# An edge-by-edge graph convolution: the loop's instruction lists are written anew, with the block's sums in two PSUM banks and a stop of the gathers for a convolution five blocks back

## The reference

```
h   = gelu(gelu(edge8 @ W_mlp1 / sqrt(8)) @ W_mlp2 / sqrt(64))     # 8 -> 64 -> 64
w00, w01, w10, w11 = h @ Wp_00, h @ Wp_01, h @ Wp_10, h @ Wp_11     # 4 x 32 radial weights
mid = products of the w's, the source node's 128 features (x[src] @ W1) and 4 edge attributes
n   = segment_sum(mid, edge_dst)                                    # per destination node
y   = c * self(x) + s * (n @ W2)
out = layernorm(x + y)
```

## Time and profile before

| | |
|---|---|
| median of 3 runs | 5393.78 us (5361.47 to 5398.54) |
| the profiled execution's own time | 5384.89 us |
| its span, first to last instruction | 5383.0 us |
| mean granted TensorE clock | 0.767 |
| PE busy | 3296.7 us (61%) |
| PE weight loads busy | 1820.5 us (34%) |
| POOL busy | 3103.5 us (58%) |
| DVE busy | 1881.7 us (35%) |
| ACT busy | 1178.5 us (22%) |

### The profile page before, as it was taken

How to read it: one execution, slowest core, us unless ns; L and a number is a source line. 1 busy time by engine, 2 the same in 40 slices (tenths; PEclk the granted TensorE clock), 3 DMA queues, 4 the chain that set the end, 5 groups by cost and what they waited for, 6 DMA issues and landing times.

```text
span 5383.0 us, 53986 instructions
## 1 busy us (share of the span) xinstructions
PE 3296.7 (61%) x15272; PEld 1820.5 (34%) x15272; DVE 1881.7 (35%) x6401; ACT 1178.5 (22%) x2646; POOL 3103.5 (58%) x3281
## 2 busy tenths in 40 slices
PE   6566655666665665666566555666666665666666
PEld 5333333333333333333333333333333333333334
DVE  2333333333333333333333333333333333333335
ACT  3222122222222221222222222222222222222224
POOL 5466555566655565556655665556565566555651
PEclk8777777777777777777777777777777787778777
DMA  6122112212212122222221221212222122122211
GB/s 152 34 47 46 44 42 44 44 44 47 46 43 46 42 46 44 44 45 45 46 45 43 47 46 42 45 44 46 43 46 45 43 46 46 43 46 45 46 45 60
DMA packets 586055, 256.02 MB, mean 48 GB/s; under 512 B 528383, under 2 KB 531867, under 8 KB 584347
## 3 DMA queue, kind: packets, MB, share of 16 engines
q0 software_dynamic: 103616, 211.52, 15.1%
q1 hardware_dynamic: 480572, 42.82, 6.7%
q10 hardware_dynamic: 1696, 0.18, 0.0%
HBM read 241.45 MB, written 12.81 MB: 47 GB/s over the span
## 4 chain that ended last, share of the span: by engine, by line
another core or an unknown queue 51%; PE 27%; issue 13%; ACT 8%; DVE 0%; ACTq 0%; DMA 0%; DVEq 0%; POOL 0%; POOLq 0%
PE bank L735 6%; PE bank L778 5%; PE bank L730 5%; PE bank L745 5%; PE bank L759 3%; PE bank L770 2%; ACT h L517 2%; ACT big L522 1%; ACT ztsb L543 1%; ACT ztsb L544 1%; PE bank L677 1%; ACT bank L532 1%; ACT idx L501 1%; ACT big L635 1%
## 5 line engine op out<-in xcount | busy, mean ns | idle before, releaser
L436 POOL DMA_INDIRECT gath<-feature_table,idx x3224 | 3077.2, 954 | 2149.6 <-issue 1711.0
L745 PE MATMUL bank<-wpbd,big 128*128 128x256 f32 x3232 | 982.4, 433 | 27.1 <-issue 25.5
L994 DVE TENSOR_TENSOR big<-bank,gath 128x256 f32<-128x256 f32 x808 | 342.2, 424 | 1737.2 <-remote 1481.8
L778 PE MATMUL bank<-ztsb,conv 128*128 128x128 f32 x1616 | 360.4, 392 | 865.4 <-ACT ztsb L544 574.8
L745 PEld LDWEIGHTS bank<-wpbd,big 128*128 128x128 f32 x3232 | 707.5, 225 | 472.5 <-issue 404.1
L997 DVE TENSOR_TENSOR big<-bank,gath 128x384 f32<-128x384 f32 x1616 | 817.9, 548 | 0.0
L770 PE MATMUL bank<-ident,zsb 128*128 128x128 f32 x1616 | 342.8, 351 | 700.3 <-issue 505.4
L735 PE MATMUL bank<-h,w2bd 128*128 128x512 f32 x804 | 571.8, 801 | 232.2 <-ACT h L517 128.0
L1022 DVE TENSOR_TENSOR acc<-acc,bank 128x8 f32 x3232 | 528.7, 164 | 509.4 <-PE bank L778 93.3
L730 PE MATMUL bank<-e8T,w1bd 128*128 128x512 f32 x804 | 571.0, 799 | 156.2 <-ACT big L522 77.6
L778 PEld LDWEIGHTS bank<-ztsb,conv 128*128 128x128 f32 x1616 | 308.1, 285 | 982.5 <-issue 492.6
(11 more groups left out here) (83 smaller groups left out, 799.0 us busy)
## 6 DMA issues: line engine op xcount, KB each, us to landing
gath<-feature_table,idx POOLq DMA_INDIRECT x3224
e<-in_edge_attr SPq DMA_DIRECT2D x416, 32.0 KB
ea_t<-in_edge_attr SPq DMA_DIRECT2D x100, 64.0 KB
feature_table<-gath SPq DMA_DIRECT2D x4, 1280.0 KB, 5.6
out<-big SPq DMA_DIRECT2D x4, 1280.0 KB
big<-in_x SPq DMA_DIRECT2D x3, 1280.0 KB, 8.4
dst_rows<-in_dst SPq DMA_DIRECT2D x1, 1536.0 KB
big<-in_src SPq DMA_DIRECT2D x1, 1408.0 KB
```

The lines of the kernel that those rows point to most:

```text
L436: pool.indirect_dma_start(out=gath[:, s % SLOTS, t, :], out_offset=None, in_=table[:, :], in_offset=bass.IndirectOffsetOnAxis(ap=idx[:, s, ...
L745: last = pe.matmul(wgt_ps[c][:, 256 * r:256 * (r + 1)], h2[:, s // SUPER % 2, s % SUPER, 16 * g:16 * (g + 1), :].rearrange("q p a -> q (p ...
L778: last = pe.matmul(y_ps, conv[:, k, :], ztsb[:, k, :], start=(k == 0), stop=(k == 3))
L994: dve.tensor_tensor(o[:, :, :, 0, :], w[:, :, :, 0, :], f[:, :, 0, :].unsqueeze(2).to_broadcast([128, n, 2, MUL]), ALU.mult)
```

## The change

- **PE** gets a list `cycle` in place of `step`. One cycle b holds, in this order: layer2 (h=1) of the block five ahead, radial chunk 2 of block b+1, layer1 (h=0) of the block six ahead, radial chunk 3 of b+1, all eight transposes of block b-1, layer2 (h=0), radial chunks 0 and 1 of b+2, the four segment sums of block b, the convolution of b-1, layer1 (h=1).
- **The sums** of a block now stand in two banks, 6 and 7 (two chunks each), and the transposes go into the same two banks. The segment sums of block b therefore wait for ACT's copies of the transposed sums of b-1.
- **Products:** those of chunks 0 and 1 alternate between `big` and `dst_rows`, which is free in the loop, so that they can be made before the previous block's are summed.
- **DVE** multiplies chunks 2 and 3 of block b and 0 and 1 of b+1, then selects for b+1, then adds the windows of block b-2. `select` reads the iota and the attributes from SBUF; ACT's copy into PSUM is gone.
- **ACT** follows the new PE list; both copies of sums and both copies of transposed sums are made together.
- **POOL** waits at the start of a block for the convolution with `s_y >= b - 5`, and before each chunk for that chunk's products four blocks back.

```diff
@@ pool
-                def gather_block(b, s, free, chunks=range(CHUNKS)):
+                def gather_block(b, s, free, b_stop, chunks=range(CHUNKS)):
                     pool.wait_ge(s_idx, b + 1)
-                    if free is not None:
-                        pool.wait_ge(s_prod[CHUNKS - 1], free)
+                    if b_stop is not None:
+                        pool.wait_ge(s_y, b_stop)
                         pool.sem_inc(s_round, 1)
                     for c in chunks:
+                        if free is not None:
+                            pool.wait_ge(s_prod[c], free)
+                            pool.sem_inc(s_round, 1)
                         gather(s, c)
@@ act
+            def cycle(b, s, group):
+                k = s + SUPER + 2
+                if s > -2:
+                    gelu1(b + (SUPER + 1), 1)
+                if s > 0:
+                    copy_sums(b - 1, 0)
+                    copy_sums(b - 1, 1)
+                if s > -2:
+                    gelu2(b + (SUPER + 1), k - 1, 1)
+                if k % SUPER == 0:
+                    copy_e8T(group)
+                gelu1(b + (SUPER + 2), 0)
+                if s > 0:
                     copy_transposed(b - 1, 0)
+                    copy_transposed(b - 1, 1)
+                gelu2(b + (SUPER + 2), k, 0)
+                if s > 0:
                     act.wait_ge(s_prod[CHUNKS - 1], b + 0)
                     copy_indices(b + (RING - 1), (s + RING - 1) % RING).then_inc(s_idx, 1)
@@ pe
+            def cycle(b, s, group, round_):
+                i, k = b + (SUPER + 2), s + SUPER + 2
+                if s > -2:
+                    layer2(b + (SUPER + 1), 1)
+                if s > -2:
+                    radial(b + 1, s + 1, 2)
+                if k % SUPER == 0:
+                    transpose_e8(k % RING, round_, i)
+                    pe.wait_ge(s_e8T, group + 1)
+                else:
+                    pe.wait_ge(s_h2[1], i)
+                layer1(k, 0)
+                if s > -2:
+                    radial(b + 1, s + 1, 3)
+                if s > 0:
+                    transpose_sums(b - 1)
+                layer2(i, 0)
+                radial(b + 2, s + 2, 0)
+                radial(b + 2, s + 2, 1)
+                if s >= 0:
+                    for c in range(CHUNKS):
+                        segment_sum(b, s, c)
+                if s > 0:
+                    convolve(b - 1)
+                pe.wait_ge(s_h2[0], b + (SUPER + 3))
+                layer1(k, 1)
@@ dve
                 dve.tensor_tensor(sel01[:, :, :], rel_all[:, ts_].unsqueeze(2).to_broadcast([128, TILES, WINDOW]),
-                                  iota_ps.unsqueeze(1).to_broadcast([128, TILES, WINDOW]),
+                                  iota_w[:, :].unsqueeze(1).to_broadcast([128, TILES, WINDOW]),
                                   ALU.is_equal).then_inc(s_sel0, 1)
...
+            def cycle(b, s, n, skipped=0):
+                if s >= 0:
+                    products(b, s, 2, n * 2 + s // SLOTS)
+                    products(b, s, 3, n * 2 + s // SLOTS)
+                if s >= -1:
+                    products(b + 1, s + 1, 0, n * 2 + (s + 1) // SLOTS - skipped)
+                    products(b + 1, s + 1, 1, n * 2 + (s + 1) // SLOTS - skipped)
+                    base = load_bases(b - 2) if s >= 2 else None
+                    select(b + 1, s + 1, (n + (s + 1) // RING) * 16 + 16)
+                if s >= 2:
+                    add_windows(b - 2, base)
```

More of the change, by code:

```diff
@@ L595, in _ @@
                 copy_odd_indices()
-                act.wait_ge(s_iop, 1)
-                lay_attributes(0, 0, 16)
-                step(0, 0, 1, 0, first=True)
+                for b in range(-2, 2):
+                    cycle(b, b, 1)
                 with act.Fori(0, ROUNDS) as n:
-                    for s in range(1, RING + 1):
-                        step(n * RING + s, s, n * 2 + (s // SUPER + 1), n + (s + 1) // RING)
-                step(BLOCKS - 1, 1, 0, 0, last=True)
-                copy_transposed(BLOCKS - 1, 0)
-                copy_sums(BLOCKS - 1, 1)
-                copy_transposed(BLOCKS - 1, 1)
+                    for s in range(2, RING + 2):
+                        cycle(n * RING + s, s, n * 2 + (s + SUPER + 2) // SUPER)
+                for pair in range(2):
+                    copy_sums(BLOCKS - 1, pair)
+                for pair in range(2):
+                    copy_transposed(BLOCKS - 1, pair)
             with act.Else():
@@ L727, in _, with layer1 @@
             pe.wait_ge(s_wts_act, 16 * (LOOP_WEIGHT_LOADS - POOL_WEIGHT_LOADS))
-            def layer1(m, h):
-                pe.matmul(hid_ps[:, :], w1bd[:, 2 * (m % SUPER) + h, :], e8T[:, :], start=True, stop=True)\
+            def layer1(k, h):
+                pe.matmul(hid_ps[:, :], w1bd[:, 2 * (k % SUPER) + h, :], e8T[:, :], start=True, stop=True)\
                     .then_inc(s_h1p[h], 1)
@@ L735, in layer2, with radial @@
                 pe.matmul(hid_ps[:, :], w2bd[:, :], h1[:, h, :], start=True, stop=True).then_inc(s_h2p[h], 1)
-            def radial(b, s, c, first=False):
+            def radial(b, s, c):
                 if c == 0 and s % SUPER == 0:
@@ L740, in radial @@
                     pe.wait_ge(s_h2[1], b + SUPER)
-                if not first:
+                if s > 0:
                     pe.wait_ge(s_prod[c], b)
@@ L1023, in add_windows @@
                         .then_inc(s_add[t], 1)
-            def step(b, s, round_, first=False, last=False):
-                base = None
-                for c in range(CHUNKS):
-                    if c == 2 and not last:
-                        select(b + 1, s + 1, None if first else b)
-                    if c == 3 and not first:
-                        base = load_bases(b - 1)
-                    products(b, s, c, round_ - (last and c < CUT_C), first)
-                if not first:
-                    add_windows(b - 1, base)
+            def cycle(b, s, n, skipped=0):
[9 more added lines that the diff above has]
+                    add_windows(b - 2, base)
             flag = dve.value_load(flag_i[0:1, 0:1], min_val=0, max_val=NODES)
```

191 lines of the change are left out of this document (68 added, 123 removed).

## The result

The change makes the kernel slower, by 1.6%: 5479.95 us (median of 4 runs, 5478.69 to 5485.16) against 5396.16 us for the kernel before in the same comparison, a ratio of 1.016 with a 95% interval of 1.0124 to 1.0196. The forecast was 5240.

A forecast was written before the change was run, and what follows sets the result against it. POOL's 16 gathers plus a pause for PE's late signals bound the kernel. Mean block 25.0 against 25.79 saves 152 us over 197.5 blocks; 5384.9 - 152 + 7 for the ends gives 5240 us, range 5090 to 5500.

The forecast's parts named there:

- What bounds the kernel: POOL's loop: 16 gathers, some 3 us until PE's late signals come, work to the last product, restart; 25.79 us a block.
- the flush: The batch in which all PE's remaining late signals come out, about 3 us after POOL stops gathering; taken at 3.1 us.
- The main term: POOL's pause a block falls to 4.3 us if the convolution has run before POOL stops; block 24.15 us.
- case D: Better rival: all is in time, blocks 24.15 and 26.0 us, total 5160, or 5090 with the flush at 2.72; chance 0.11.
- The deciding point: Whether PE's convolution has run before the flush: R+21.3 against R+22.95 (R is POOL's restart), 1.6 us to spare; block 24.6 us.
- the term for the segment sums: PE's four segment sums at the low clock take about 4.0 us (0.64 warm), ahead of the convolution's 2.1.
- my walk: The new cycle timed step by step from a flush, POOL restarting 1.2 us later (R); the convolution has run at R+21.3.
- Rival A: Slower: the second transposes' signal misses the flush, such blocks take 30.8 us; at one in three 5645 us; chance 0.20.
- The fourth blocks: Every fourth block has e8 transposes and their copy ahead of layer1: 1.4 us becoming about 4, block 26.3, bounds 25 and 29.
- Ends: One step more after the last gather, +11.7 us; at the start one product needed instead of four, -5.
- Edits at nothing: DVE's adds, POOL's three added waits, ACT's dropped attribute copy and SP's loads waiting for select: all priced at no cost.
- rival C: DVE's select with two SBUF inputs and POOL's gathers shut each other out: up to 1.0 us a block, 5432; chance 0.07.

The follow-up runs named there:

- seg_wide: Changed kernel with segment sums as 2 double-width matmuls a chunk, not 4 (part of the sums wrong): 5366.98 us, 0.9725 of the kernel before, PE's signals late.
- conv_layer_e8: Changed kernel with e8 rows loaded early, PE's convolution and second layer1 ahead of the segment sums: 5563.59 us, 1.0303 of the kernel before, PE's signals late.
- e8_early: Changed kernel with SP loading e8 rows ahead of its wait for select: 5565.73 us, 1.0092 of the kernel before, PE's signals late.
- no_stop: Changed kernel without POOL's wait for the convolution, its four chunk waits kept: 5425.44 us, 1.0073 of the kernel before, PE's signals late.

## Why the prediction was wrong, by its own steps

- **What bounds the kernel** (16 gathers, some 3 us to the flush, work behind it, restart) held in every kernel with signals held. My 25.79 us a block counted the last block as if a pause followed it; block by block it is 25.81.
- **The main term** was right: a block whose convolution is in time takes 24.1 us in the recorded kernel, and 24.0 to 24.3 in seg_wide, conv_layer_e8 and the others; I had 24.15. With half the instructions for the sums and no late rows three of the four pauses shown above are 3.8 to 4.9 us, and the time is 0.948 of the kernel before, near case D.
- **The deciding point failed, at the term for the segment sums.** I let the four sums take 4.0 us with PE free to issue, and so the convolution run at R+21.3. Up to there PE and its signals were even earlier than in my walk: the late layer2 ends at R+7.1 (medians of the blocks between; I had R+8.25), its signal comes at R+11.3 and not R+17, and the sums start at R+9.1 and not R+15.2. But they end at R+21.7 and not R+19.2: 12.6 us in place of 4.0, because PE stops at some 64 to 70 instructions whose signals have not come, and there are 100 between that layer2 and the end of the convolution. My walk priced each held signal for the engine that waits for it, and put a stop of PE itself at nothing. The convolution is in time in 14% of the blocks between, and these blocks take 25.53, not 24.6: 0.93 x 148 = 138 us.
- **Rival A**, a signal of the transposes held to the flush, is what the fourth blocks do (R = 2235.43; 49 of 49), and what the two kernels with the convolution moved did in most blocks, at 26 to 29 us and not 30.8. In the blocks between of the recorded changed kernel it was never the cause, so the loss there is described by none of my rivals. That 5480 lies inside the 5090 to 5500 that I gave is luck: the upper part of that range stood there for rivals whose mechanism the blocks between don't show.
- **The fourth blocks** were mis-sized: 28.39, not 26.3, 2.1 x 49 = 103 us. I wrote that SP's loads wait for `select` in place of ACT's copy, 8 blocks ahead, and priced it at nothing. SP's e8 loads stand behind that same wait, and the new list turns e8 six blocks ahead, not four. But e8_early shows that this wait alone wasn't the cause: take it away, and held signals of the transposes take its place. Either cause alone keeps a fourth block at 28.5 to 29.9 us; both gone gives 25.3.
- **Ends:** the stretch behind the last gather grew by 15.6 us, where I had 11.7, and the first gather with a wait starts 0.6 us sooner, where I had 5: 8 us more.
- **The sum:** 138 + 103 + 8 = 249, and 5240 + 249 = 5489, 4 us above the profiled execution's 5485.16. These 4 are the 0.02 us a block of the first point.
- **Edits at nothing:** DVE's adds and POOL's four chunk waits stayed covered, but for one stop of 7.3 us ahead of a third chunk at the start of the loop.
- **The lock between DVE and POOL** (rival C) is there, and I took nothing for it. I had priced it at up to 1.0 us a block. It cost 11.5 us of gather time in the whole recorded run, since a gather is lengthened only where it starts while L972 runs, and 20.0 us with signals free. The Trainium skill, "SBUF — State Buffer", section "SBUF: two separate sides", has this rule; the trace agrees for gathers that start during L972 (1.47 us against 0.95), but L972 itself doesn't wait (694 ns, where L986 took 686). No run undid this edit alone.

## What to carry to other kernels

Where an engine's signals come late, its instruction count between two releases is a resource of its own: count loads and matmuls ahead of the signal that others need before the durations are added up, and read "issue" gaps inside a group that waits for nothing as that count being used up. Fewer, wider matmuls then paid although they stream the same columns, and here a new order of the same instructions only chose which of them was late. When a list is rewritten to run further ahead, follow each DMA queue's own waits to the new due time, and expect two causes to mask each other: test them together as well as alone, and see whether the wait that was taken away has come back at another place. And where VectorE instructions get a second input in SBUF beside indirect DMAs, look for single long gathers: the mean (958 ns against 954) hides them.

## What the runs showed that I had not expected

- Signals held or free is no property of the kernel: the kernel before took 4197 us and 5521 us on the same chip in two comparisons. With signals held the recorded changed kernel's trace has 10,016 changes of the gathers' semaphores (the kernel before 9,719), with signals free the same kernel's has 51,023, for the same 3,224 gathers of 16 increments each. That the increments are taken in bunches and PE's behind them would fit; no run here shows it.
- PE stops with mostly 64 to 70 loads and matmuls out whose signals have not come.
- The release comes about 3 us behind POOL's last gather before the pause in every kernel with signals held (medians of 2.7 to 2.9 us), wherever in the block the pause lies (no_stop pauses ahead of chunk 2).
- A gather that starts while `select` reads two inputs in SBUF takes up to 1.48 us in place of 0.95.
